# Twelve attention layers and a gated FFN: ScalarE's weight conversions, a register read and one wait of TensorE are moved

## The reference

```
for i in range(12):
    q, k, v = split(x @ Wqkv[i].T + bqkv[i])
    y = (q @ k.T * scale) @ v              # per batch and head
    x = y @ Wproj[i].T + bproj[i] + x
x = layernorm(x0 + x)
h = silu(x @ wg.T) * (x @ wu.T)            # wg, wu, wd = w_int / 127
x = layernorm(x + h @ wd.T)
```

## Time and profile before

| | us |
|---|---|
| median of 3 runs | 312.1 (311.68 to 312.29) |
| the profiled execution, its own time | 311.1 |
| its span | 309.2 |
| TensorE busy | 302.2 (98%) |
| VectorE busy | 226.4 (73%) |
| ScalarE busy | 194.8 (63%) |
| GpSimd busy | 123.7 (40%) |

### The profile page before, as it was taken

The page is one execution under the profiler, slowest core; times in us unless marked ns, Lnnn a source line. Parts: engine busy times, 40 slices in busy tenths (PEclk is TensorE's granted clock), DMA queues, the critical chain, the costliest instruction groups (busy, mean ns, idle before and its releaser), DMA issues.

```text
span 309.2 us, 9537 instructions
## 1 busy us (share of the span) xinstructions
PE 302.2 (98%) x3951; PEld 281.6 (91%) x3951; DVE 226.4 (73%) x688; ACT 194.8 (63%) x481; POOL 123.7 (40%) x118
## 2 busy tenths in 40 slices
PE   8999999999999999999999999999999999999993
PEld 8989999899898998999989999999898789999982
DVE  0477587776876878758778587786875987887873
ACT  3449578497595775966749668587595275444550
POOL 3036242371443623525136152360545454656442
PEclk9999999999999999999999999999999999999999
DMA  7603020030020300303003010020000000111112
GB/s 269 260 2 112 6 101 14 4 112 2 13 105 2 115 1 5 112 2 107 11 2 115 3 59 21 4 80 2 2 2 2 2 1 3 54 50 34 37 34 72
DMA packets 8908, 14.96 MB, mean 48 GB/s; under 512 B 800, under 2 KB 5280, under 8 KB 8864
## 3 DMA queue, kind: packets, MB, share of 16 engines
q1 hardware_dynamic: 8144, 13.34, 13.0%
q10 hardware_dynamic: 720, 0.99, 0.9%
HBM read 12.23 MB, written 2.10 MB: 46 GB/s over the span
## 4 chain that ended last, share of the span: by engine, by line
PE 96%; DVE 2%; issue 0%; POOLq 0%; POOL 0%; ACT 0%
PE ps L964 14%; PE ps L1085 14%; PE ps L1033 8%; PE ps L1202 7%; PE ps L920 7%; PE ps L921 6%; PE ps L922 6%; PE ps L1001 5%; PE ps L983 4%; PE ps L1191 4%; PE ps L1190 4%; PE ps L1025 3%; PE ps L937 2%; PE ps L1162 2%; PE ps L990 2%; PE ps L975 2%
## 5 line engine op out<-in xcount | busy, mean ns | idle before, releaser
L448 POOL TENSOR_TENSOR step_lo<-step,step_hi 128x512 fp32r<-128x512 f32 (+1 forms) x44 | 52.2, 1219 | 42.6 <-ACT step_hi L556 42.6
L419 POOL TENSOR_TENSOR wq_lo<-w,wq_hi 128x512 fp32r<-128x512 f32 x12 | 15.3, 1275 | 99.7 <-ACT wq_hi L533 99.7
L920 PE MATMUL ps<-state_hi,step_hi 128*128 128x258 f32 x165 | 47.4, 287 | 0.3 <-issue 0.3
L922 PE MATMUL ps<-state_hi,step_lo 128*128 128x258 f32 x165 | 46.7, 283 | 0.0
L921 PE MATMUL ps<-state_lo,step_hi 128*128 128x258 f32 x165 | 46.6, 283 | 0.0
L964 PE MATMUL ps<-w,gram 128*128 128x128 f32 x352 | 42.8, 275 | 0.0
L964 PEld LDWEIGHTS ps<-w,gram 128*128 128x128 f32 x352 | 41.9, 192 | 0.6
L529 ACT COPY gk<-ps 128x512 f32<-128x512 f32 x48 | 28.1, 586 | 20.6 <-PE ps L964 20.6
L1085 PE MATMUL ps<-step,gram 128*128 128x128 f32 x320 | 38.7, 279 | 0.0
L1085 PEld LDWEIGHTS ps<-step,gram 128*128 128x128 f32 x320 | 36.8, 191 | 0.8
L576 ACT COPY gram<-ps 128x256 f32<-128x256 f32 x88 | 32.8, 373 | 4.7
(11 more groups left out here) (140 smaller groups left out, 630.4 us busy)
## 6 DMA issues: line engine op xcount, KB each, us to landing
w<-weights SPq DMA_DIRECT2D x12, 592.5 KB, 3.8
xchan<-x_chan SPq DMA_DIRECT2D x8, 256.0 KB, 4.1
out<-xchan SPq DMA_DIRECT2D x7, 256.0 KB, 2.3
xt<-x_tok SPq DMA_DIRECT2D x4, 258.0 KB, 5.1
xt<-x_tok ACTq DMA_DIRECT2D x3, 258.0 KB, 5.4
fw_int<-ffn_weights SPq DMA_DIRECT2D x1, 576.0 KB, 5.3
cst<-consts SPq DMA_DIRECT2D x1, 147.5 KB, 6.7
xt<-x_tok SPq DMA_DIRECT2D x1, 129.0 KB, 2.7
```

The costliest lines, as they stand in the source:

```text
L448: nc.gpsimd.tensor_tensor(split_group(step_lo, g), split_group(step, g), split_group(step_hi_f, g), ALU.subtract).then_inc(step_lo_ready, 1)
L920: nc.tensor.matmul(dst, l_hi, r_hi, start=True, stop=False)
L922: return nc.tensor.matmul(dst, l_lo, r_hi, start=False, stop=True)
```

## The change

Three edits. ScalarE's conversions of the FFN weights stand in another place of the layer, directly behind the copy of the query weights and ahead of the wait for `s`, and the down weights' scaling has moved from layer 2 to layer 3; VectorE's two steps on the down weights each stand a layer later. TensorE reads the flag behind `gk_stage(3)` and no longer behind `s_stage`. And `a_stage(0)` waits for the first half of step group 0 ahead of batches 0 and 1, and for the second half ahead of batches 2 and 3, where before it waited for both.

```diff
                 nc.scalar.copy(wq_hi[:, :], w[:, s, WQ:WQ + QUADS * P]).then_inc(wq_hi_ready, 1)
+                if at(1, 0) == FW_LAYER:
+                    act.wait_ge(fw_in, 16)
+                    nc.scalar.copy(fw[:, 0:2 * HIDDEN], fw_int[:, 0:2 * HIDDEN]).then_inc(ffn_chain, 1)
+                if at(1, 0) == FW_LAYER + 1:
+                    act.wait_ge(ffn_chain, 1)
+                    nc.scalar.copy(wgu_hi[:, :], fw[:, 0:2 * HIDDEN]).then_inc(ffn_chain, 1)
+                if at(1, 0) == FW_LAYER + 2:
+                    nc.scalar.mul(fw[:, 2 * HIDDEN:], fw_int[:, 2 * HIDDEN:], SCALE_W).then_inc(wd_scaled, 1)
                 act.wait_ge(s_done, at(2, 1))
...
-                if at(1, 0) == FW_LAYER:
-                    act.wait_ge(fw_in, 16)
-                    nc.scalar.copy(fw[:, 0:2 * HIDDEN], fw_int[:, 0:2 * HIDDEN]).then_inc(ffn_chain, 1)
-                if at(1, 0) == FW_LAYER + 1:
-                    act.wait_ge(ffn_chain, 1)
-                    nc.scalar.copy(wgu_hi[:, :], fw[:, 0:2 * HIDDEN]).then_inc(ffn_chain, 1)
-                    nc.scalar.mul(fw[:, 2 * HIDDEN:], fw_int[:, 2 * HIDDEN:], SCALE_W).then_inc(wd_scaled, 1)
...
-                if at(1, 0) == FW_LAYER + 2:
+                if at(1, 0) == FW_LAYER + 3:
                     dve.wait_ge(wd_scaled, 1)
...
-                if at(1, 0) == FW_LAYER + 3:
+                if at(1, 0) == FW_LAYER + 4:
                     dve.wait_ge(wd_meaned, 1)
...
                 gk_stage(3)
+                if last_layer:
+                    low_parts()
                 pe.wait_ge(b_lo_ready, at(PAIRS, PAIRS))
...
                 s_stage((1, 2, 3), S_REST, GROUPS)
-                if last_layer:
-                    low_parts()
                 n_first()
...
                 for b in range(GB * g, GB * (g + 1)):
+                    if g == 0 and b % 2 == 0:
+                        pe.wait_ge(step_ready, STEPS * (LAYERS - 1) + b // 2 + 1)
                     left = b_whole[:, b - SPLIT, :] if b >= SPLIT else bsum[:, b, :]
...
-            pe.wait_ge(step_ready, STEPS * (LAYERS - 1) + 2)
             a_stage(0)
```

## The result

The first six runs of the changed kernel have a median of 309.84 us (309.51 to 310.58), six of the kernel before 312.08 (311.62 to 312.29): ratio 0.9934, 95% interval 0.9919 to 0.9949.

The account below looks back on a forecast made before the run. The prediction took TensorE to bound the kernel (96% of the chain), with four pauses to remove. Its terms, 0.71 - 0.02 + 0.33 + 0 + 0.30 = 1.32 us, took the median from 312.1 to 310.8 us, range 310.3 to 311.6.

Parts of the forecast that it names:

- ScalarE's conversions: Layers 1 and 2 fall to 19.90 us; the new place in ScalarE's pause costs 0; gain 0.71 us.
- The second rival: Conversions take half as long again and make `s_rows` late; gain 0.8 us at worst, time 311.3; 9 in 100.
- VectorE in layer 5: Moved step uses up VectorE's 0.54 us pause ahead of `mt`; lateness 0 to 0.05, taken as -0.02 us.
- The flag's old place: Last layer, ahead of `n_first`: removing the read saves 0.37 us, of which 0.33 reach `step`.
- Its new place: Last layer, ahead of L975: read starts near 232.3, through by 233.3, hidden by the `kdiag` wait; cost 0.
- The first rival: Flag's read waits until the array runs dry, L975 1.00 us late; gain 0.32, time 311.8; 6 in 100.
- the slower one: Read drains the array and the pause halves TensorE's clock to 1.2 GHz; time 317.9 us; 2 in 100.
- The first A products: Last layer: products start on the first half of `step`, so `a_cent` comes 0.28 to 0.34 earlier; taken 0.30 us.
- One sign of being wrong: Time from `a_cent` to the end of the span longer than 65.6 us by more than 0.1.
- The sum: All edits over the whole kernel: 0.71 - 0.02 + 0.33 + 0 + 0.30 = 1.32 us.
- The number for the first six runs: Median of the changed kernel: 312.1 - 1.3 = 310.8 us, 0.42% less.
- The width: Range of 310.3 to 311.6 us, covering the forecast, a median's shift of perhaps 0.3 and conversions that do not fit.

Follow-up runs that it names:

- the further copy: Changed kernel with one more copy of 512 columns on ScalarE ahead of the weights' rounding in layer 2; one execution, 310.30 us.
- the spreading: Kernel before with ScalarE's conversions in their old place but one to a layer, VectorE's two steps a layer later; one execution, 312.02 us.
- the experiment behind `kdiag`: Changed kernel with the flag's read moved behind the wait for `kdiag`, ahead of `m_means()`; ratio 0.9959.
- the 28 later runs: Changed kernel, unedited, run again in three sets of 12, 9 and 7; common median 310.72 us.
- the further sets: Both kernels run again unedited; medians 312.09 and 312.19 us for the kernel before, 310.72, 311.11 and 310.60 for the changed one.

## Why the prediction was right and where it was wrong

**ScalarE's conversions** were right: 0.71 forecast, 0.7 measured in the two windows, each step of the way in its row. The Trainium skill's "Advanced Engine Details and Errata", section "The Read-Write Bubble", does not add to the durations in this trace: in the changed kernel and in two experiments (the further copy, and the spreading) ScalarE's next instruction starts 0.09 to 0.10 us before the written end of the last. The second rival, conversions that do not fit, is out.

**VectorE in layer 5** was right in that the pause is just used up; the lateness of 0.02 that I had put into the sum is not there (layer 5 takes 19.88 to 19.91 us in the four traces of the changed kernel, 19.91 before).

**The flag's old place** was right: 0.33 forecast, 0.34 measured alone. **Its new place** cost nothing, as forecast, but one step of the reasoning failed. I had the read start near 232.3, as soon as the means were there; the changed kernel has it at 232.5 with the last layer's products 0.72 earlier, so it is 233.2 on the scale of the kernel before. The sequencer is ahead of the array, but at 232.5 four or five of the 20 loads of L964 had gone in since 232.00, at 0.12 each, so 15 or 16 loads, about eight matmuls, stood between it and the array. With 0.93 us for the read, it ends 0.2 ahead of `kdiag` and not 1.1. It was still enough, and the experiment behind `kdiag` shows that even that wait was not needed. The first rival (the read drains the array) is out, and with it the slower one: there is no pause, and the granted clock is 1.00 in this stretch too, as the window from the last layer's first product to the first A product shows:

```profile
230.61:241.04 10.43, 10.39 (x214) 9.20 (x213) 6.96 (x20) 5.19 (x13) 6.48 (x6) 1.00 0.01 3
```

The prediction says that no row of this case shows a fall of the clock after idle time. That holds only as long as TensorE has work. Behind its last product it stands idle to the end of the span, and there the granted clock of the changed kernel goes from 1.00 to 0.76 and 0.50, which is the 1.2 GHz level:

```profile
304.00:305.00 1.00, 0.00 (x0) 0.00 (x0) 0.29 (x1) 0.40 (x1) 0.41 (x1) 1.00 0.21 61
305.00:306.00 1.00, 0.00 (x0) 0.00 (x0) 0.00 (x0) 0.00 (x0) 0.00 (x0) 0.76 0.67 187
306.00:308.00 2.00, 0.00 (x0) 0.00 (x0) 0.00 (x0) 0.00 (x0) 0.00 (x0) 0.50 0.07 17
```

It costs nothing there, as no product follows, and it does not tell what a pause of 1 us would have done.

**The first A products** were right: 0.30 forecast, 0.30 measured alone, and `a_cent` took over directly from step group 1 as written. Their loads start 0.14 us behind L943's where I had 0.08. One sign of being wrong that I had named did come: from `a_cent` to the end of the span it is 65.86 us and not 65.6. The sign was ill chosen, since it holds the end, and the kernel before fails it too (65.87 and 66.74 in its other traces). From `a_cent` to ScalarE's last instruction it is 62.19 to 62.21 us in all seven traces of the two kernels, so the whole gain lasts.

**The sum** was right: 1.32 us forecast, 1.32 measured as the mean stretch of four traces against three; the 28 later runs have a median of 310.72 against 310.8 forecast. It rests on a plain layer of 19.90; the views on record ahead of the prediction have windows of layers 3 to 7 only, and the chain's starts give 19.90, 19.94 and 19.88 for layers 8 to 10, so layer 6 does stand for them.

**The number for the first six runs was wrong**, and the step that failed is not a term of the sum but how it was carried to the median. Two sentences did it: the profiled execution "lies 1.0 us under the median", kept as a constant, and "a median moves by perhaps 0.3". For the profiled execution I had 309.8, and it took 309.86. But the median of its six runs was 309.84 and not 1.0 us higher. That offset was itself scatter: over the further sets of the two kernels the profiled execution lies between 0.02 us under and 0.52 over its median, and with one edit alone it was once 0.43 over and twice 0.8 under. The warning was in the first profile, whose execution took 311.1 us, 0.6 below the lowest of the three runs shown. The width was too small as well: the kernel before did keep within 0.3 (medians of 311.87 to 312.19 in its sets), but the changed kernel has 309.84, 310.60, 310.72 and 311.11. Single executions of the kernel before scatter over 2.3 us (92 runs, 310.88 to 313.22), all of it in start and end as far as the traces show. Why the first six fell 0.9 us under the later ones stays open. In hindsight 309.8, the profiled execution's own forecast, would have been the low end. The sign, and the 1.32 us of the edits, were not touched by it.

## What to carry to other kernels

On an engine that runs beside the bound, an extra instruction costs its delay less the slack of the place where it stands: the same conversion of 768 columns cost nothing in front of a wait and 0.16 us in its old place, and with a second one behind it 0.55. A register read on TensorE costs its latency of about 0.9 us less the matmuls already issued, so it belongs behind a run of long products. And where a gain of a few tenths of a per cent is to be judged, measure in the traces from the first to the last instruction of the part in question: three traces gave that part to 0.1 us where medians of 6 to 12 runs were off by up to 0.9.

## What the runs showed of the hardware that I had not expected

- How far TensorE's sequencer runs ahead: when the flag's read began, 15 or 16 loads of 128 x 128 were still to go in (0.12 us each) in the changed kernel, and 20 or 21 loads of 32 x 128 in the kernel before (24 from 237.19 at 0.03 each, the read at 237.3). It is eight to ten matmuls in both.
- The first transfers and the last one move single executions, the start by up to 1.06 us and the end by up to 1.16: the start took 11.43 to 12.49 us and the end 3.42 to 4.58 in fourteen traces, while the 294 us in between repeat to 0.1 us.
